# Rows of a mixture of experts turned by a transposing DMA instead of TensorE, and the collect stage moved into the head of the gather stage

## What is computed

```python
xn = layernorm(x)
x = x + segment_sum(edge_weight[:, None] * xn[dst], src) @ W.T + b   # graph part
      + linear_attention(xn)                                         # 8 heads, elu + 1 features
n = layernorm(x)
g = n @ Wg.T + bg                       # 8 experts, the two best of each row
for e in range(8):                      # combine: softmax over the two, 0 elsewhere
    out += combine[:, e:e+1] * (relu(n @ W1[e].T + b1[e]) @ W2[e].T + b2[e])
return x + out
```

## Time and profile before

| | us |
|---|---|
| median of 3 runs (2059.4, 2065.72, 2065.83) | 2065.72 |
| the profiled execution | 2061.87 |
| its span | 2060.1 |
| collect, and the head of graph up to the first product | 273 to 293 |
| graph's gathers | 287 to 1314 |
| route | to 1442 |
| experts | 1442 to 2060 |

### The profile page before, as it was taken

One profiled execution on the slowest core, in us unless ns is written; L12 is line 12 of the kernel. 1 busy time (PEld: TensorE's weight loads), 2 busy tenths in 40 slices (PEclk: granted clock), 3 DMA queues, 4 the chain that ended last, 5 costly groups with the idle time before them and its releaser, 6 DMA issues. The chain is left out here.

```text
span 2060.1 us, 51259 instructions
## 1 busy us (share of the span) xinstructions
PE 1679.4 (82%) x15514; PEld 1307.2 (63%) x15514; DVE 1576.0 (77%) x3328; ACT 1427.1 (69%) x4087; POOL 1264.0 (61%) x1229
## 2 busy tenths in 40 slices
PE   5677658888888789888886666563899999999998
PEld 2466546666666577777764444342677777777776
DVE  8899839888898899999998889886455555555554
ACT  6565448887788788888878878565556666666564
POOL 3377747777777777777777777650344444444443
PEclk9899979999999999999999999755999999999999
DMA  6022345555555544444433356360232222322221
GB/s 221 27 77 88 96 154 162 155 158 157 159 159 151 154 144 124 125 125 123 120 106 103 102 161 192 125 205 5 63 50 45 48 50 47 49 49 48 49 46 29
DMA packets 140382, 219.02 MB, mean 106 GB/s; under 512 B 32086, under 2 KB 97536, under 8 KB 140002
## 3 DMA queue, kind: packets, MB, share of 16 engines
q0 software_dynamic: 62816, 134.68, 25.6%
q1 hardware_dynamic: 70950, 74.70, 11.7%
q10 hardware_dynamic: 6364, 6.40, 0.9%
HBM read 172.28 MB, written 44.36 MB: 105 GB/s over the span
## 5 line engine op out<-in xcount | busy, mean ns | idle before, releaser
L1018 POOL DMA_INDIRECT misc<-z_d,consts x814 | 779.1, 957 | 271.2 <-issue 167.2
L1254 DVE SCALAR_TENSOR_TENSOR acc<-ps,consts,acc 128x512 f32 x814 | 609.1, 748 | 73.7 <-PE ps L1341 56.5
L1041 ACT ACTIVATE misc<-misc 128x256 f16<-128x256 f16 x872 | 390.9, 498 | 79.6 <-DVE misc L1121 75.2
L1848 ACT ACTIVATE misc<-ps,misc 128x128 f32<-128x128 f32 x840 | 239.4, 368 | 239.6 <-PE ps L1813 165.2
L1339 PE MATMUL ps<-misc 128*128 128x256 f16 x1088 | 298.6, 274 | 111.7 <-ACT rec L1041 37.1
L1889 POOL DMA_INDIRECT out<-misc,pos x105 | 166.1, 1582 | 289.6 <-ACT misc L1913 254.0
L1813 PE MATMUL ps<-misc,big 128*128 128x128 f16 x1680 | 327.6, 220 | 0.0
L1811 PE MATMUL ps<-misc,big 128*128 128x128 f16 x1680 | 327.2, 220 | 0.1
L1812 PE MATMUL ps<-misc,big 128*128 128x128 f16 x1680 | 326.5, 219 | 0.0
L1828 PE MATMUL ps<-big,rec 128*128 x840 | 320.2, 382 | 0.0
L1341 PE MATMUL ps<-misc 128*128 128x256 f16 x1088 | 299.0, 275 | 0.0
(11 more groups left out here) (349 smaller groups left out, 3775.5 us busy)
## 6 DMA issues: line engine op xcount, KB each, us to landing
big<-in_w2T SPq DMA_DIRECT2D x60, 256.0 KB, 2.9
misc<-z_d,consts POOLq DMA_INDIRECT x814
big<-xT_d SPq DMA_DIRECT2D x98, 128.0 KB
big<-in_w1T SPq DMA_DIRECT2D x32, 256.0 KB, 2.9
tok_d<-misc SPq DMA_DIRECT2D x50, 132.0 KB, 1.8
xT_d<-misc SPq DMA_DIRECT2D x49, 128.0 KB
z_d<-misc SPq DMA_DIRECT2D x49, 128.0 KB, 1.7
acc<-in_x SPq DMA_DIRECT2D x6, 896.0 KB
```

The costliest lines, as they stand in the source:

```text
L1018: e.indirect_dma_start(out=rows[n % RB], out_offset=None, in_=c.z_d, in_offset=bass.IndirectOffsetOnAxis(ap=idx[u][:, k:k + 1], axis=0)).t ...
L1041: e.activation(hot[n % HG][:, half, :], same[n % OG], ACT.Copy, scale=near[n // UG % 3][:, t % UG, 1 + half:2 + half]).then_inc(s_hot, 1)
L1254: e.scalar_tensor_tensor(out=rows_of, in0=out_ps[tile % BG], scalar=c.gain, in1=rows_of, op0=ALU.mult, op1=ALU.add).then_inc(s_add, 1)
L1848: l = e.activation(hidden[:, m, :], h_ps[u][:, m, :], ACT.Relu, bias=b1x[u][:, m:m + 1])
```

## The change

**Experts.** `turn`, its PSUM tiles and ScalarE's copy are gone. SyncE issues one transposing DMA for each tile, `xs` to `xT`, both in SBUF, as soon as the gather has landed and `first` has finished with the buffer's last contents. `xs` and `xT` have 4 buffers each instead of 2, and lie in the accumulator's memory, which is free by then. The gather of a tile waits for the transposing DMA that read its buffer. In `second`, the waits for the next step are issued ahead of the second matmul of the present step (`ready`), or in the last step behind its last matmul.

**Collect.** The block is gone. Three areas are loaded in rank as before. The fourth is loaded by the first two DMAs of graph's SyncE program, at another place in SBUF. TensorE turns the table in three parts (tiles 0 to 127, 128 to 639, 640 to 815); ScalarE takes out the first part and fetches the first 24 tiles' indices before it takes out the other two. VectorE numbers the parts ahead of the bias and the first indicator.

```diff
@@ build
-        with nc.cleanup_on_exit():
-            collect(nc, c)
@@ rank, SyncE
-            for m in range(AR):
+            for m in range(AR - 1):
                 e.wait_ge(s_sc[m], 16 * KG * (NG // AR))
...
-            e.wait_ge(s_areas, 32 * AR)
+                area_in(e, c, m, s_areas)
+            e.wait_ge(s_areas, 32 * (AR - 1))
@@ graph
+    CUT = [(0, P), (P, 5 * P), (5 * P, ET)]
         @block.sync
+            area_in(e, c, AR - 1, s_area)
+            e.dma_start(c.pos[0:1, :], c.blk_d).then_inc(s_blk, 16)
             e.dma_start(wk, A["kv_wT"][:, :, 0:D]).then_inc(s_w, 16)
@@ graph, ScalarE
+            def evicted(x):
+                a, b = CUT[x]
+                e.wait_ge(s_part, 4 * x + 1)
+                e.copy(q_i[:, a:b], parts[x][1]).then_inc(s_ids, 1)
+                for k in (2, 3):
+                    e.wait_ge(s_part, 4 * x + 1 + k)
+                    e.copy(marks[:, a:b, k], parts[x][k]).then_inc(s_share, 1)
             e.wait_ge(s_ones, 5)
+            evicted(0)
+            e.wait_ge(s_mark, 2)
+            e.wait_ge(s_share, 2)
             fetch(0)
             fetch(1)
+            evicted(1)
+            evicted(2)
+            e.wait_ge(s_mark, 6)
+            e.wait_ge(s_share, 6)
@@ graph, VectorE (numbered: L837 to L842 for one part)
+            for x in range(len(CUT)):
+                numbered(x)
+            e.wait_ge(s_mark, 6)
+            e.wait_ge(s_blk, 16)
             e.wait_ge(s_bias, 1)
@@ graph, TensorE (gathered: L817 to L823 for one part)
+            e.wait_ge(s_area, 32)
+            for x in range(len(CUT)):
+                gathered(x)
+            e.wait_ge(s_ids, 3)
+            e.wait_ge(s_share, 6)
+            e.wait_ge(s_mark, 6)
@@ experts
-    def turn(e, i):
-        u = i % 2
-        e.wait_ge(s_xs[u], 16 * (i // 2 + 1))
-        if i >= 2:
-            e.wait_ge(s_xt, i - 1)
-        for n in range(2 * DH):
-            l = e.transpose(tr_ps[u][:, n, :], xs[u][:, n * P:n * P + P], c.ident16)
-        l.then_inc(s_tr, 1)
@@ first
         if m == 0:
-            e.wait_ge(s_xt, i + 1)
+            e.wait_ge(s_xt[i % XB], 16 * (i // XB + 1))
+    def ready(e, n):
+        i, m = n // HB, n % HB
+        if i < MT and m % half == 0:
+            e.wait_ge(s_low, 2 * i + 1 + m // half)
+        if i < MT and m == 0 and i >= 2:
+            e.wait_ge(s_t, i - 1)
@@ second
-        if m % half == 0:
-            e.wait_ge(s_low, 2 * i + 1 + m // half)
-        if m == 0 and i >= 2:
-            e.wait_ge(s_t, i - 1)
...
         l = e.matmul(y_ps[u], high[u][:, m, :], c.w2[:, bass.ds(at, 2 * D)], start=m == 0, stop=m == HB - 1)
+        if m == HB - 1:
+            l.then_inc(s_out, 1)
+        ready(e, i * HB + m + 1)
         if m < HB - 1:
             e.matmul(y_ps[u][:, 0:D], low[u][:, m, :], c.w2[:, bass.ds(at, D)], start=False, stop=False)
@@ experts, SyncE
+            for i in range(MT):
+                k = i % XB
+                e.wait_ge(s_xs[k], 16 * (i // XB + 1))
+                if i >= XB:
+                    e.wait_ge(s_h, 2 * (i - XB + 1))
+                e.dma_start_transpose(xT[k], xs[k][:, 0:2 * D]).then_inc(s_xt[k], 16)
@@ experts, GpSimd
+            def gather(i):
+                k = i % XB
+                if i >= XB:
+                    e.wait_ge(s_xt[k], 16 * (i // XB))
+                    e.wait_ge(s_p, i - XB + 1)
@@ experts, ScalarE
-                e.copy(xT[u], tr_ps[u]).then_inc(s_xt, 1)
-                e.copy(shares[u], xs[u][:, 2 * D:ROW].bitcast(F32)).then_inc(s_p, 1)
+                e.wait_ge(s_xs[i % XB], 16 * (i // XB + 1))
+                e.copy(shares[u], xs[i % XB][:, 2 * D:ROW].bitcast(F32)).then_inc(s_p, 1)
```

More of the change, by code:

```diff
@@ L198, in rank @@
     assert ring.at <= NB * EC // 2
[L199 to L205, removed]
+    assert big.at - 4 * D <= AREA_AT
+    c.loaded = [matrix(c.big[:, at:at + AREA].bitcast(F16), TR, P * PC) for at in (
+        AREA_AT, AREA_AT + AREA, AREA_AT + 2 * AREA, AREA_AT - AREA)]
     prod32 = [p.bitcast(I32).rearrange("p n (k c) -> p n k c", c=SC) for p in prod]
@@ L917, in graph @@
     idx = c.idx
+    CUT = [(0, P), (P, 5 * P), (5 * P, ET)]
+    late = Arena(c.big, AREA_AT - AREA)
+    late.at = AREA_AT - AREA - 2 * ET
+    q_i, dst_i = (late.take(ET, I32) for _ in range(2))
+    parts = [[c.bank[(4 if x == 1 else 0) + k][:, 0:b - a] for k in range(PC)] for x, (a, b) in enumerate(CUT)]
+    s_area, s_blk, s_part, s_ids, s_shift, s_mark, s_share = map(S, ("area", "blk", "part", "ids", "shift", "mark", "share"))
     first = lambda q: isinstance(q, int) and q == 0
@@ L1762, in experts @@
     more.t = c.rec[:, :].bitcast(F32)
-    xs = [misc.take(ROW, F16) for _ in range(2)]
-    xT = [matrix(misc.take(2 * D, F16), 2 * DH, P) for _ in range(2)]
-    b2 = c.acc[:, 0:NE * D]
+    XB = 4
+    spare = Arena(c.acc, NB * BR * D // P)
+    b2 = spare.take(NE * D)
+    xT = [matrix(spare.take(2 * D, F16), 2 * DH, P) for _ in range(XB)]
+    xs = [spare.take(ROW, F16) for _ in range(XB)]
     shares, weight = [misc.take(NE) for _ in range(2)], [misc.take(1) for _ in range(4)]
@@ L1773, in experts @@
     S = lambda name: c.sem("experts_" + name)
-    s_b, s_bias, s_bx, s_tr, s_xt, s_h, s_relu, s_high, s_low, s_out, s_y2, s_y = map(S, (
-        "b1", "bias", "b1_x", "tr", "xt", "h", "relu", "high", "low", "out", "y2", "y"))
+    s_b, s_bias, s_bx, s_h, s_relu, s_high, s_low, s_out, s_y2, s_y = map(S, (
+        "b1", "bias", "b1_x", "h", "relu", "high", "low", "out", "y2", "y"))
     AHEAD, LAG = 6, HB + HB // 2
-    s_xs, s_ys, s_t, s_p, s_wt, s_b2 = [S("xs0"), S("xs1")], [S("ystore0"), S("ystore1")], S("sum"), S("shares"), S("weight"), S("b2")
-    tr_ps = [matrix(c.bank[u][:, 0:D].bitcast(F16), 2 * DH, P) for u in range(2)]
+    s_xs, s_xt = [S(f"xs{k}") for k in range(XB)], [S(f"turned{k}") for k in range(XB)]
+    s_ys, s_t, s_p, s_wt, s_b2 = [S("ystore0"), S("ystore1")], S("sum"), S("shares"), S("weight"), S("b2")
     h_ps = [matrix(c.wide[1 + u], HB, P) for u in range(2)]
@@ L1893, in _ @@
             for i in range(AHEAD):
-                gather(Step(i // 2, i % 2))
+                gather(i)
             for i in range(MT):
@@ L1950, in _ @@
             x = {}
-            turn(e, 0)
             for n in range(MT * HB + LAG):
```

70 lines of the change are left out of this document (44 added, 26 removed).

## The result

The changed kernel takes 2044.6 us in the median of 4 runs (2041.56 to 2046.29), the kernel before beside it 2065.77 us (2059.4 to 2066.12). The ratio is 0.9903, 95% interval 0.9881 to 0.9926. Forecast were 2023 us: the sign is right, and of the 43 us between the forecast and the median before 21 came (the forecast's own sum, reckoned from the profiled execution, was 38.7). The profiled execution took 2045.16 us, with a span of 2043.5.

A forecast was written before the change was run, and what follows sets the result against it. TensorE was taken to bound experts, GpSimd's gathers graph. Terms -23.6 - 7.9 + 1.5 - 8.7 = -38.7 us, from the profiled 2061.87 us, gave 2023 us; forecast 2012 to 2034, full range 2010 to 2056.

The forecast's parts named there:

- The bound of experts: Experts: TensorE, busy 199.05 of 200 us, is the limit, so whatever leaves its stream shortens the stage as much.
- The transposes leave, 23.6 us: Experts: four transposes per tile leave TensorE, 0.225 us a tile over 105 tiles, 23.6 us gained.
- The waits move, 7.9 us: Experts, step m = 0: two waits moved behind the 512-column matmul L1828 are hidden, 0.075 us a tile, 7.9 us gained.
- the low bound, nothing: Experts: the moved waits gain nothing if they then delay the next matmul as much.
- The transposing DMA, 3.0 us: Experts: each 128 KB transposing DMA takes 3.0 us, with its latency covered and its rate within the 5.4 us per tile.
- The start of the stage: Experts, tile 0: TensorE's first L1811 comes 1.5 us later because of the transposing DMA, bounds 0.3 and 5.
- The rivals that make it or the add to `out` the limit: First, chance 0.14: transposing DMA limits experts, 2149 us. Second, 0.07: adds' landing lengthens to 5.4 us or more, 2053 us.
- the third: Rival, chance 0.03: waits change places in graph, transposes' time reappears as waits for the DMA, about 2062 us.
- The upper bound of 6.6 us: Experts: a transposing DMA moving 32-byte pieces would have 4096 packets at 26 ns over 16 engines, 6.6 us.
- The head of graph, 8.7 us: Graph: TensorE and VectorE run 6.9 us ahead, GpSimd moves up 1.8 more, 8.7 us gained, bounds 6.9 and 10.9.
- exactly the term: Head of graph: the first gather goes at about 276.1 instead of 287.00, 10.9 us earlier.

The follow-up runs named there:

- one_wait: Changed kernel without TensorE's waits for the relu and the total, VectorE taking the total of tile i-2 ahead of its split of tile i: 2024.45 us, ratio to before 0.9815.
- pause: Changed kernel with four transposes of the identity, without waits and with unread results, put back where the tile's transposes stood: 2042.94 us, experts stretch 585.0 us.
- pause_fewer: one_wait with four bare transposes of the identity put back: experts stretch 576.1 us, ratio to before 0.9897.
- before_less_one: Kernel before without the second of the two waits ahead of its transposes, transposes staying on TensorE: experts stretch 585.4 us, ratio to before 0.9946.
- waits_back: Changed kernel with the waits of `second` put back to where they stood before: 2043.83 us, experts stretch 584.0 us.
- twice: Changed kernel with every transposing DMA issued twice, the second into a buffer nobody reads: 2045.66 us, experts stretch 586.4 us.
- head_only: Kernel before with collect in the head of graph alone, experts as before: ratio to before 0.9992, experts stretch 597.8 us.
- exp_only: Kernel before with the changed experts stage alone, collect staying its own block: ratio to before 0.9945, experts stretch 583.9 us.

## Why the prediction was right or wrong

**The bound of experts: wrong, and the root of the rest.** The prediction read 199.05 us busy in 200 as "whatever is taken out of TensorE's stream shortens the stage by as much". With fixed addresses the same matmuls and transposes need 574.1 us instead of 597.5. The busy time counts matmuls that overlap, and stretched ones as much as dense ones: it is 198.49 us in the changed kernel and 198.64 in one_wait, which is 18 us shorter. (The Trainium skill says so, in "Perfetto Trace Analysis", at its head: matmul busy time is a bad metric because matmuls are pipelined. This trace agrees.) The sequencer's rows were there to be read. In the kernel before, too, the commonest distance between two address computations is 0.125 us, and there are 40 and three waits per tile.

**The transposes leave, 23.6 us: wrong.** Their price on the array was right (22.6 us with fixed addresses). On the path they are worth 1.1 us in the changed kernel (pause), 4.7 us with one wait instruction more, and 10.2 us once the queue has room (pause_fewer). Most came instead from what the sum had put at nothing, the wait instruction that stood before them: 12.1 us (before_less_one), or 8.9 if the transposes leave first. I had not counted the waits of the step that leaves.

**The waits move, 7.9 us: wrong.** The step "they stand behind L1828 ... and are hidden" failed; the low bound, nothing, was right (waits_back). I had read the 0.13 us of the earlier trace rows as a cost of the place. It is a cost of the number: there are two waits at that place, so one is an instruction.

**The transposing DMA, 3.0 us: right.** 2.9 us from issue to TensorE's start. The start of the stage came out at +1.3 us, from the block's first gather to the first weight load (1438.81 to 1446.57; before 1443.27 to 1449.70), against +1.5. The rivals that make it or the add to `out` the limit are refuted: the gather lands in 2.9 us and the add in 3.8, as in the earlier trace rows, and twice the number adds 2.5 us to the stretch. Nor did the transposes' time come back as a wait for the DMA (the third): TensorE waits for it once. The upper bound of 6.6 us took 4096 packets for each; the pages count 57,120 more on the hardware queue than before, 544 for each. The 1309 ns per block of the Trainium skill ("VectorE: DVE Perf Modes", The three transpose paths) would as an estimate be 10.5 us for the eight blocks of a tile in twice; they pass in 5.6. As a price of one block among many it doesn't hold here.

**The head of graph, 8.7 us: right in mechanism, too large, by how much is open.** Measured from the start of the turning, which itself moves by 5 us between executions, the first gather came 10.9 us sooner (2.95 us against 13.8 and 13.9), exactly the term. The 21st came 38.9 and 39.2 us behind it before and 31.3 to 32.1 in eight executions after: 7.2 us sooner, where 8.7 were expected. The turning itself began 1.6 us later in the mean (273.6 against 272.0), and from the 21st gather to the last the changed kernel took 1002.2 us in the mean of eight against 1000.7 and 1000.4. Together 4.0 us at the last gather. Two executions of before are too few to say whether the last two pieces, 3.2 us, belong to the change; their spread of 2.5 us says no more than that they may not. The medians point higher. Both profiled executions of before are below the median of the runs beside them, by 3.9 and 2.2 us. Take from the difference of the medians what experts gave, its stretch and the 1.3 us at its start. The seven changed kernels with several executions on such chips then leave 5.2 to 8.9 us, 6.9 in the mean. An estimate of 4 to 7 us is what the runs bear out, against 8.7.

On the slower kind of chip the head is worth less. In head_only TensorE's turning is broken by idle times for which the trace shows no wait (timeline):
```profile
282.72 7.64 PE L1353 MATMUL ps<-consts,big 128*128 128x128 f16 x89 [18.94 <-DMA big<-rec_d]
...
294.30 0.43 PE L1353 MATMUL ps<-consts,big 128*128 128x128 f16 x3 [0.95 <-issue]
...
296.43 0.47 PE L1353 MATMUL ps<-consts,big 48*128 48x48 f16 x3 [1.20 <-issue]
...
300.34 1.19 PE L1364 MATMUL ps<-big 2*128 2x256 f32 x2 [2.42 <-ACT rec L1074]
```
The bias matmul, which waits for the last part, starts 17.6 us after the turning, against 10.6 in the profiled execution above (271.10 to 281.73). Gathers started 10.6 us sooner than in exp_only and then stood before a first product that came no sooner (303.36; exp_only, with the old head, 301.72). Why the turning is broken there isn't shown.

**Sum.** Forecast -23.6 - 7.9 + 1.5 - 8.7 = -38.7. Measured in the pair of traces: experts -13.6 + 1.3, and -4.4 at its first gather (1443.27 to 1438.81): -16.7, which is the difference of the profiled executions (2061.87 to 2045.16). The medians differ by 21.2. The shortfall is nearly all in experts: -12.3 instead of -30.0.

## What to carry to other kernels

Before pricing an instruction taken off a full-looking TensorE, count what its sequencer does per tile: register work for addresses and waits with a row of their own. If these fill the tile, matmuls with constant addresses can be nearly free, and the cheap edit is to drop implied waits. Taking out one redundant wait here gave nearly what moving all transposes to a DMA gave, and dropping two more in the changed kernel gave another 19.7 us (0.9815 of before). Put waits apart: one at a place rides on the next instruction, the second costs an instruction.

## What the runs showed of the hardware that I had not expected

- Addresses of weight or moving tiles that are computed from a register follow each other at 0.125 us in TensorE's sequencer, the matmuls handed on between them included; 40 of them take 5.0 us, and with no wait instruction left the stage still takes 565.9 us where the array needs 551.5. What makes up the rest of the 5.41 us tile wasn't attributed.
- A wait instruction that is long satisfied has a duration of 51 ns and costs 85 to 89 ns when the sequencer is the limit and the tile has no transposes; with transposes one in each of the 103 tiles cost between 4.3 and 12.1 us in all. (The Trainium skill has 50 to 100 ns for reading a semaphore from a sequencer, in "Advanced Engine Details and Errata", Network/Comms. The 51 ns fit that; whether such a wait is one reading, no run here shows.)
- Four transposes with constant operands, 0.22 us of array time, cost 0.01 us per tile in the changed kernel, whose sequencer is behind, and 0.10 us where it has no wait instruction.
- A transposing DMA of 128 KB took SyncE 1.19 us to issue and 2.9 us from issue to TensorE's start on its data, and two per 5.6 us pass beside gathers and accumulating stores.
